# Two-layer feed-forward stage: five blocks a layer made into one, the token shift by transfers between partitions

## The reference

```python
x = x + 0.5 * L0_ffn(layernorm(x));  x = x + L0_attn(layernorm(x));  x = x + 0.5 * L0_ffn(layernorm(x))
def shift_token(t):            # features 64..127 come from the token before, 0 for the first of a sequence
    t1, t2 = split(t, 2);  return concatenate([t1, pad(t2, one token in front)[:, :-1]])
def _layer(x, ...):            # L0_ffn: two of these
    q, k, v = split(shift_token(x) @ wqkv, 3)            # 8 heads of 64
    q, k = rotary_xpos(l2norm(q) * qs, l2norm(k) * ksc)
    x = x + local_attention(q, k, v) @ wo                # windows of 64 tokens, each with the one before
    h = shift_token(x);  h = (h - mean) / sqrt(var + 1e-5) * lg + lb
    a, g = split(h @ w1 + b1, 2)                         # 341 and 341
    return x + (a * gelu(g)) @ w2 + b2
```

## Time and profile before

| | us |
|---|---|
| median of 3 runs (lowest, highest) | 2824.32 (2814.48, 2829.72) |
| profiled execution: its time | 2822.83 |
| profiled execution: span of the core | 2821.1 |
| PE busy, DVE busy, ACT busy, POOL busy | 2263.1, 1529.8, 1201.7, 359.0 |
| mean granted clock of PE, share of full speed | 0.887 |

### The profile page before, as it was taken

One profiled execution on the slowest core, in us unless ns is written; L12 is line 12 of the kernel. 1 busy time (PEld: TensorE's weight loads), 2 busy tenths in 40 slices (PEclk: granted clock), 3 DMA queues, 4 the chain that ended last, 5 costly groups with the idle time before them and its releaser, 6 DMA issues. The chain is left out here.

```text
span 2821.1 us, 44016 instructions
## 1 busy us (share of the span) xinstructions
PE 2263.1 (80%) x17129; PEld 1236.0 (44%) x17129; DVE 1529.8 (54%) x2700; ACT 1201.7 (43%) x2076; POOL 359.0 (13%) x545
## 2 busy tenths in 40 slices
PE   3987897796977987897899999798548668980498
PEld 2664564473654664344222222344336544440244
DVE  4963893656954873215688786311844582128610
ACT  2763674254753773222377777421224322230121
POOL 2320330213311320000000000000010000003000
PEclk9998898898988998899699999999777778995699
DMA  3000000001000000000100110000001100000000
GB/s 121 2 2 0 1 2 1 5 3 43 2 1 0 2 2 1 23 0 32 57 22 24 27 27 2 8 1 4 0 8 27 45 1 8 0 0 0 0 0 15
DMA packets 20191, 36.49 MB, mean 13 GB/s; under 512 B 8770, under 2 KB 11074, under 8 KB 19362
## 3 DMA queue, kind: packets, MB, share of 16 engines
q1 hardware_dynamic: 19858, 32.93, 3.7%
q0 software_dynamic: 144, 0.96, 0.2%
HBM read 27.88 MB, written 4.46 MB: 11 GB/s over the span
## 5 line engine op out<-in xcount | busy, mean ns | idle before, releaser
L1738 DVE TENSOR_REDUCE fa_top<-psum 128x1 f32<-128x1024 f32 x256 | 304.6, 1221 | 84.9 <-PE psum L1683 84.2
L1727 ACT ACTIVATE fa_prob<-psum 128x512 f32<-128x512 f32 x512 | 278.7, 596 | 118.0 <-PE psum L1696 116.9
L471 DVE TENSOR_TENSOR scaled<-psum,area_b 128x512 f32<-128x512 f32 x16 | 11.1, 692 | 472.6 <-PE psum L436 472.6
L429 PE MATMUL psum<-hidden_b,area_b 128*128 128x512 f32 x512 | 221.0, 592 | 0.0
L429 PE MATMUL psum<-hidden_a,area_b 128*128 128x512 f32 x512 | 221.0, 592 | 0.0
L1696 PE MATMUL psum<-fa_stack_q,fa_stack_k 74*128 74x512 bf16 x512 | 199.4, 393 | 10.9 <-ACT fa_prob L1727 5.1
L1683 PE MATMUL psum<-fa_stack_k,fa_stack_q 72*128 72x512 bf16 x512 | 204.4, 408 | 3.8 <-DVE fa_top L1738 2.9
L589 POOL TENSOR_TENSOR turn_a<-turn_a,turn_b 128x1024 f32<-128x1024 f32 x64 | 151.1, 2361 | 266.2 <-DVE turn_b L773 266.2
L600 PE MATMUL psum<-area_a,zt 128*128 128x512 f32 x256 | 143.9, 689 | 35.5 <-ACT k_t L712 14.8
L429 PEld LDWEIGHTS psum<-hidden_a,area_b 128*128 128x128 f32 x512 | 97.3, 190 | 122.5 <-issue 122.5
L429 PEld LDWEIGHTS psum<-hidden_b,area_b 128*128 128x128 f32 x512 | 97.3, 190 | 122.5 <-issue 122.5
(11 more groups left out here) (327 smaller groups left out, 4443.1 us busy)
## 6 DMA issues: line engine op xcount, KB each, us to landing
area_b<-in_L_ffn SPq DMA_DIRECT2D x2, 2888.0 KB, 9.9
fa_stack_q<-fa_parts_dram SPq DMA_DIRECT2D x144, 32.0 KB
fa_stack_k<-fa_parts_dram SPq DMA_DIRECT2D x144, 32.0 KB
area_a<-in_L_ffn SPq DMA_DIRECT2D x1, 4402.0 KB, 13.0
fa_parts_dram<-fa_prob SPq DMA_DIRECT2D x12, 256.0 KB, 2.6
area_b<-in_L_attn SPq DMA_DIRECT2D x1, 1880.5 KB, 16.7
area_a<-in_L_attn SPq DMA_DIRECT2D x1, 1538.0 KB, 6.8
wa_q_rows<-area_a SPq DMA_DIRECT2D x64, 16.0 KB
```

What stands on the lines that cost most here:

```text
L429: last = nc.tensor.matmul(psum[:, 4 + n % 2, :], w(name)[:, k * TF_HID + m * P:k * TF_HID + (m + 1) * P], src[:, c, k, :], start=(k == 0), ...
L1727: nc.scalar.activation(prob[:, (2 * s + j) % RING, half * CHUNK:(half + 1) * CHUNK], psum[:, 4 + n % 2, :], ACT.Exp, scale=float(D) ** -0. ...
L1738: nc.vector.tensor_reduce(top[:, g % 2, j, t:t + 1], psum[:, 2 * j:2 * j + 2, :].rearrange("p a n -> p (a n)"), AX.X, ALU.max, negate=True ...
```

## The change

`l0_ffn` becomes one block for both layers. `local_attention`'s steps stay, with `g = l * 16 + n` in their counts. `glu`, `unshift`, the second `first_tokens`, and the second and third `normalise_block` go, and the first one runs for layer 0 alone. The token shift of the feed-forward is made by two transfers per chunk on SP: partitions 0 to 126 of y's upper halves to partitions 1 to 127 of `moved`, and partition 127 to partition 0. Statistics are taken of the two halves apart and merged. The steps of the gated unit are written into the order in which the attention's last tiles end, and in layer 0 also the transposes for layer 1 and the first steps of its tile 0. `x` is updated chunk by chunk in layer 1's tail. The turned tile 0 of each layer goes to the score banks.

```diff
+        def sp_shift(sp, l, c):
+            at, end, done = c * PER_CHUNK, (c + 1) * PER_CHUNK, shifts[c % 2].handle
+            fresh = c * CHUNK % SEQ == 0
+            sp.wait_ge(*added.at(l * TILES + end))
+            sp.dma_start(moved[1:P, at:end, :], y[0:P - 1, at:end, HALF:P]).then_inc(done, 16)
+            sp.dma_start(moved[0:1, at + fresh:end, :], y[P - 1:P, at - 1 + fresh:end - 1, HALF:P]).then_inc(done, 16)
+            shifted_chunk(sp, l, c)
+        def dve_stats(dve, l, c):
...
+            shifted_chunk(dve, l, c)
...
+            for j in range(PER_CHUNK):
+                nc.vector.bn_stats(stats[:, j, 0, :], y[:, c * PER_CHUNK + j, 0:HALF])
+                last = nc.vector.bn_stats(stats[:, j, 1, :], moved[:, c * PER_CHUNK + j, :])
...
+            for j in range(PER_CHUNK):
+                last = nc.vector.bn_aggr(moments[:, c % 2, j, :], stats[:, j])
...
+            nc.vector.tensor_scalar(spread[:, c % 2], moments[:, c % 2, :, 1], 1e-5, None, ALU.add)
+        def dve_normalise(dve, l, c):
+            for j in range(PER_CHUNK):
...
+                nc.vector.tensor_scalar(tokens[:, c % 2, j, 0:HALF], y[:, c * PER_CHUNK + j, 0:HALF], mean, scale, ALU.subtract, ALU.mult)
+                last = nc.vector.tensor_scalar(tokens[:, c % 2, j, HALF:P], moved[:, c * PER_CHUNK + j, :], mean, scale,
+                                               ALU.subtract, ALU.mult)
+        def pe_up(pe, l, c, m):
...
+                pe.wait_ge(*gated.at(l * UPS + u - 1))
```

More of the change, by code:

```diff
@@ L739, in act_take_v @@
+            p, after, made = g % 3, (g + 1) % 3, v_bank.rearrange("p (h d) -> p h d", h=H)
             nc.scalar.copy(v[:, p, 1, :, 0:D], made)
@@ new lines, in pe_turn_tokens, with act_take_tokens @@
+        def pe_turn_tokens(pe, l, c):
+            q = l * CHUNKS + c
+            pe.wait_ge(*normed.at(q + 1))
+            if c < 2:
+                pe.wait_ge(*qk_taken.at((l + 1) * TILES))
+            else:
+                pe.wait_ge(*taken.at(q - 1))
+            for j in range(PER_CHUNK):
+                last = nc.tensor.transpose(psum[:, c % 2, j * P:(j + 1) * P], tokens[:, c % 2, j, :], core.ident[:])
+            last.then_inc(turned.handle, 1)
+        def act_take_tokens(act, l, c):
+            act.wait_ge(*turned.at(l * CHUNKS + c + 1))
+            nc.scalar.activation(ht[:, c * CHUNK:(c + 1) * CHUNK], psum[:, c % 2, :], ACT.Identity, bias=w(f"lb{l}"),
+                                 scale=w(f"lg{l}")).then_inc(taken.handle, 1)
@@ new lines, in pe_up @@
+        def pe_up(pe, l, c, m):
+            u, (at, rows) = c * M + m, GLU_PARTS[m]
+            pe.wait_ge(*taken.at(l * CHUNKS + c + 1))
+            if u == 0:
+                pe.wait_ge(*shifted_s.at((l + 1) * TILES))
+            elif u == 1:
+                pe.wait_ge(*o_ready.at((l + 1) * TILES))
+            else:
+                pe.wait_ge(*gated.at(l * UPS + u - 1))
+            for part in range(2):
+                last = nc.tensor.matmul(pair(u)[0:rows, part, :], w(f"w1{l}")[:, part * GLU_HID + at:part * GLU_HID + at + rows],
+                                        ht[:, c * CHUNK:(c + 1) * CHUNK], start=True, stop=True)
+            last.then_inc(up.handle, 1)
@@ new lines, in pe_down @@
+        def pe_down(pe, l, c):
+            pe.wait_ge(*gated.at(l * UPS + (c + 1) * M))
+            if c == 0:
+                pe.wait_ge(*v_taken.at((l + 1) * TILES))
+            elif c == 1:
+                pe.wait_ge(*added.at((l + 1) * TILES))
+            else:
+                pe.wait_ge(*fed.at(l * CHUNKS + c - 1))
+            if l == 0 and c == 3:
+                pe.wait_ge(*next_taken.at(2))
+            w2 = w(f"w2{l}")
+            for j in range(PER_CHUNK):
+                for m, (at, rows) in enumerate(GLU_PARTS):
+                    last = nc.tensor.matmul(down_bank(c)[:, j * P:(j + 1) * P], hidden[0:rows, c % 2, m, j * P:(j + 1) * P],
+                                            w2[0:rows, m * P:(m + 1) * P], start=(m == 0), stop=(m == M - 1))
+            last.then_inc(low.handle, 1)
```

698 lines of the change are left out of this document (438 added, 260 removed).

## The result

The changed kernel took 2703.16 us in the median of 4 runs (2699.50 to 2709.09), the kernel before 2824.86 beside it (4 runs, 2814.48 to 2829.72). The ratio is 0.9576, 95% interval 0.9544 to 0.9608. Forecast were 2716 and a range of 2684 to 2750. The profiled execution has a span of 2697.7 us, 123.4 less than before, and a mean granted clock of 0.903.

What follows compares the result with a forecast made beforehand. PE and DVE were taken as nearly full in the attention, with engines taking turns in four stretches after it. 57.2 us a stage, twice, less 10 for clock, plus 2 for layer starts, from 2822.8 gave 2716, range 2684 to 2750.

Steps and rivals of the forecast that it cites:

- The transfer: Chunk 3's token shift after add 15: 508 pieces on one engine at 18 ns each, 10.9 us, bounds 7.9 and 16.2.
- The wait: DVE idle before `stats 3` in each tail, about 6 us, until the transfer of chunk 3 lands.
- The rival with the spread transfer: Chunk 3's transfer spread over the engines takes 2.3 us, 5.8 less in each of four tails: 2693 us; chance 0.17.
- The slopes: Kernel loses 4 us per us of transfer; from 16.6 us on chunk 2 is late too, then 8.
- The slower rival: Each piece served after the one before: no gain at 50 ns a piece, 2864 us at 60 ns; chance 0.06.
- PE sets the time from gate 1 2 on: After gate 1 2 at 228.0, PE's products set each end's length; gains 34.0 us in layer 0, 23.2 in layer 1.
- The working's ends: Schedule from add 15: layer 0 to tile 1's normalisation at 262.5, layer 1 to x complete at 249.0.
- The clock, -10 us: PE's stands in each tail drop its clock to the lower level, costing 2.5 us a tail, 10 off the gain.
- Add 15, 0.6 us late: At the attention's end, work on chunks 0 to 2 fits DVE's idle time; add 15 ends at 210.3 against 209.7.
- The forms of 64 columns: DVE's half-column statistics and normalisation, 3.4 us per chunk; at the 128-column price 1.0 more each, 2730 us.
- Start of a layer, +2: Turned tile 0 has its own banks, so PE need not wait for tile 1's rotary: 0.5 us gained a layer.

Runs made afterwards that it cites:

- e1_spread: Changed kernel with the 127-row transfer cut into 112 and 15 rows, dealt over 16 and 15 DMA engines: 2689.21 us, ratio 0.9528.
- e4_doubled: Changed kernel with the 508 pieces of each 127-row transfer sent once more, first, into a spare buffer: 2737.07 us, ratio 0.9696.
- e7_quad: Changed kernel with the 508 pieces of each transfer sent four times, three of them first into a spare buffer: 2859.41 us, ratio 1.0128.
- e6_end_first: Changed kernel with the work on chunks 0 to 2 put behind add 15 instead of between the attention's last adds: 2731.67 us, ratio 0.9681.
- e8_spread_late: Changed kernel with the transfer split into 112 and 15 rows and chunk 3's statistics placed later: 2693.42 us, ratio 0.9538.
- e9_spread_end_first: Changed kernel with the work on chunks 0 to 2 behind add 15 and the transfer split into 112 and 15 rows: 2735.27 us, ratio 0.9695.

## Why the prediction was right, step by step

**The transfer.** One engine: right (one completion). 18 ns a piece, taken from the straight line between 128 and 512 B: too dear, 14.2 in steady flow, so 9.3 us in place of 10.9, inside the bounds of 7.9 and 16.2. The rows behind the price were busy shares, and by that measure this transfer has 18.4 ns a packet (last section), so the straight line was right; the error was to take busy time for the pace. It is worth 1.6 us in each of four ends, 6.4.

**The wait.** DVE's idle time before `stats 3` was forecast at about 6 us, released by the DMA: 4.3 to 4.4 in the four ends, less by the earlier landing. It is worth 4.4 us an end (e1_spread). The rival with the spread transfer gave 2693; the kernel built that way took 2689.

**The slopes.** 4 us per us of transfer up to 16.6, then 8: measured 4.7 (4.2 by the ends alone) and 8.5. At 16.5 us chunk 2 was just not late (e4_doubled), at 30.9 it was (e7_quad). No faster than before was forecast for 27.1 us; between the two runs the line reaches 2823 at 16.5 + 86 / 8.5 = 26.6. The slower rival was a real mechanism whose condition, 50 ns a piece, was 3.5 times away.

**PE sets the time from gate 1 2 on.** The working's ends, from the start of add 15 (210.0) to the marks, were 52.5 and 39.0. With the 9.3 us transfer they are 50.9 and 37.4; measured are 50.1 and 37.5. This is the step on which most of the gain rested.

**The clock, -10 us: wrong.** 2.5 us were taken for each of four ends. The fall came inside the unit in two of them, the first and the fourth (the window 219 to 228 with 0.81 shows the first), and cost PE 1.8 us there; in the other two PE did up 2 0 in 1.96 at full clock. Yet the ends are equal with and without it: 50.09 and 50.16 in layer 0, 37.53 and 37.60 in layer 1. It fell on up 2 0 and the transposes of chunk 3, which lie beside DVE's statistics and normalisation; the product after them began at 226.44, where the working with a 9.3 us transfer has 228.0 - 1.6 = 226.4. Slow PE work beside the chain that sets the time cost nothing here.

**Add 15, 0.6 us late: wrong in size.** It came 2.3, 3.8, 2.5 and 1.1 later after add 11 than before; e6_end_first takes it back to 23.5 in every layer. The rest of the scatter follows the clock. Where the granted clock between the two adds was 0.92 or 0.93, they lie 23.4 to 23.6 us apart before and 25.9 to 26.1 in the changed kernel; where it was 1.00, 22.3 before (second layer) and 24.5 in the changed kernel (fourth). At like clock the interleaving costs 2.2 to 2.6 us in every layer; 3.8 and 1.1 come from the clock having been full on one side only. The forms of 64 columns are not the cause: statistics, merges and epsilon of a chunk measure 1.67 us, the normalisation 1.78, together 3.45 for the 3.4 taken. PE's rows show most of it. Between `turn_o` and `out` it used to stand 0.73 us for ACT's copy; an up product of 1.72 stands there now:

```profile
206.58 0.66 PE L723 MATMUL psum<-ident,o 128*128 128x128 f32 x4 [0.39 <-DVE y L884]
207.07 1.88 PE L969 MATMUL psum<-glu_in,area_a 128*128 128x512 f32 x4
208.79 1.05 PE L733 MATMUL psum<-area_a,o_t 128*128 128x128 f32 x8
```

From `turn_o` to `out` it takes 2.21 us instead of 1.39 (205.68 - 204.29 in e6_end_first), 0.8 more each for tiles 14 and 15, 1.6 of the 2.5 in this layer. Another 0.6 is there by add 13 (16.93 us after add 11, 16.32 in e6_end_first), where the forecast had 0.4 for `shift 15`. No run moves the up products alone, so this split is read from the rows. Against it stand ends that are 8.6 to 8.9 us shorter than those of e6_end_first, so the trade is a good one.

**Start of a layer, +2.** From tile 1's mark to add 11 the attentions are 1.5, 1.0 and 1.3 us shorter and once 0.1 longer: 3.7 for the 2 taken. The stretch that got longer had a lower clock than before (0.99 against 1.00). That the free banks are the cause was tested by no run.

**The sum again**, against the 123.4 us between the two spans: 106.4 forecast, +6.4 for the transfer, +10 for the clock, -7.3 for add 15 (9.7 in place of 2.4), +1.7 for the start of a layer, +2.1 because the third stage's ends had been that much longer before than the first's, from which the forecast was made, and 2.9 elsewhere in the span, whose place is open: 122.2. The errors were larger than the 13 us by which the forecast was off, and partly cancelled; that it came so near is in part luck.

## What to carry to other kernels

Count the rows of a transfer's outermost dimension before costing it: 127 rows went on one engine and 112 + 15 on sixteen and fifteen, for one instruction more. If the transfer can't be split, order its first reader behind other work on the same engine; either takes the wait away, and with enough work in between the speed of the transfer was worth nothing (e8_spread_late, e9_spread_end_first). When filling idle time in a chain between engines, compare the filler with the single gap it goes into: 1.7 us in a 0.7 us gap made each step of the chain 0.8 us longer, although the engine stood in many other places. And before calling 2 us between two stretches an effect of the order, set their granted clocks side by side.

## What the runs showed of the hardware that was not expected

The issue of the second, four-piece transfer kept SP for 6.4 us (211.00, above), where the first took 0.70; in e7_quad, whose SP timeline follows, each transfer behind the first took 6.5 to 7.2 us to issue, close to the 7.2 us of 508 pieces.

```profile
226.50 0.68 SPq L905 DMA_DIRECT2D spare_halves<-y  x1
227.22 6.55 SPq L906 DMA_DIRECT2D spare_halves<-y  x1
233.81 7.04 SPq L907 DMA_DIRECT2D spare_halves<-y  x1
240.89 7.20 SPq L908 DMA_DIRECT2D moved_halves<-y  x1
```

So SP's next issue lasts about as long as the transfer before it flows on its one engine; what holds it, no run here shows. With the 127 rows spread (e1_spread) the three issues took 0.66, 0.88 and 0.72 us. In this stretch nothing else was queued on SP, and the last of the four pieces is moved right behind the 508, so it cost nothing.

The pieces' busy share is no measure of their rate: 2.2% of 27 us on 16 engines over 517 packets is 18.4 ns a packet, while they followed one another every 14.2 ns.
